# Expert and router products of a two-layer language tower in full float32, the two weight matrices in the two row halves of the TensorE array

## What is computed

```python
flat = _rmsnorm(x, ln2_w).reshape(-1, Cx)                 # 2048 rows of 64
probs = jax.nn.softmax(flat @ router_w.T, axis=-1)        # 8 experts, the best 2 are kept
...
for e in range(NE):                                       # NE = 8, w1, w3: 170 x 64, w2: 64 x 170
    hh = jax.nn.silu(flat @ w1[e].T) * (flat @ w3[e].T)
    out = out + weights[:, e:e + 1] * (hh @ w2[e].T)
```

## Time and profile before

| what | us |
|---|---|
| median of 3 executions (328.81 to 329.77) | 328.85 |
| the profiled execution, own time | 330.29 |
| its span, first to last instruction | 328.5 |
| TensorE busy (89% of the span) | 292.5 |
| VectorE busy (71%) | 233.4 |
| ScalarE busy (45%) | 148.3 |
| GpSimd busy (36%) | 118.0 |
| data moved by transfers | 15.24 MB |

### The profile page before, as it was taken

The page is one execution under the profiler, slowest core; times in us unless marked ns, Lnnn a source line. Parts: engine busy times, 40 slices in busy tenths (PEclk is TensorE's granted clock), DMA queues, the critical chain, the costliest instruction groups (busy, mean ns, idle before and its releaser), DMA issues.

```text
span 328.5 us, 4420 instructions
## 1 busy us (share of the span) xinstructions
PE 292.5 (89%) x1556; PEld 166.5 (51%) x1567; DVE 233.4 (71%) x428; ACT 148.3 (45%) x249; POOL 118.0 (36%) x168
## 2 busy tenths in 40 slices
PE   1649989999989999889999999989999999999873
PEld 1315754753423444467655555555564555557552
DVE  1578788889989778567864687844768677675476
ACT  2113634752566677755547444544533111021283
POOL 5774000331661235301412550430105589930212
PEclk9999999999999999979999999999999999999996
DMA  7958300285000000700000000000000000000001
GB/s 249 335 108 351 167 0 0 42 156 94 3 2 2 2 3 1 257 0 2 1 0 0 3 0 2 0 0 0 3 0 0 2 0 0 1 2 0 0 3 64
DMA packets 6270, 15.24 MB, mean 46 GB/s; under 512 B 1384, under 2 KB 3816, under 8 KB 5608
## 3 DMA queue, kind: packets, MB, share of 16 engines
q1 hardware_dynamic: 5685, 14.41, 14.5%
q0 software_dynamic: 512, 0.53, 0.7%
q10 hardware_dynamic: 51, 0.01, 0.0%
HBM read 12.01 MB, written 0.52 MB: 38 GB/s over the span
## 4 chain that ended last, share of the span: by engine, by line
PE 52%; DVE 9%; POOL 4%; ACT 4%; issue 3%; another core or an unknown queue 0%; POOLq 0%; DVEq 0%; ACTq 0%
PE ps L336 48%; DVE arena L1893 1%; PE ps L837 1%; DVE h L2020 1%; POOL share L600 1%; ACT L1217 1%; PE ps L1110 1%; PE ps L881 1%; POOL share L601 1%; ACT arena L1396 1%; DVE xs L1820 0%; POOL rw L493 0%; DVE h L2069 0%; DVE xc L2081 0%
## 5 line engine op out<-in xcount | busy, mean ns | idle before, releaser
L1759 DVE TENSOR_REDUCE rw<-ps 128x1 f32<-128x512 f32 (+2 forms) x80 | 45.8, 628 | 6.9 <-PE ps L336 6.4
L1336 ACT ACTIVATE arena<-ps 128x1024 f32<-128x1024 f32 (+3 forms) x48 | 37.6, 812 | 23.8 <-PE ps L336 23.3
L336 PE MATMUL ps<-arena 96*128 96x512 bf16 (+7 forms) x192 | 43.1, 327 | 0.5 <-DVE rw L1759 0.2
L336 PE MATMUL ps<-xs,e_hi 128*128 128x512 f32 x96 | 40.5, 422 | 1.0 <-ACT arena L1396 0.8
L1396 ACT ACTIVATE arena<-ps 128x512 f32<-128x512 f32 x48 | 28.5, 597 | 28.1 <-PE ps L336 23.8
L1893 DVE TENSOR_TENSOR arena<-ps,arena 128x512 f32<-128x512 f32 x48 | 32.4, 686 | 11.3 <-ACT arena L1396 9.8
L336 PE MATMUL ps<-xs,e_lo 128*128 128x512 f32 x96 | 37.9, 395 | 0.0
L336 PE MATMUL ps<-bfc_s 128*128 128x512 bf16 (+2 forms) x100 | 27.5, 345 | 1.8 <-DVE xc L1616 1.6
L336 PEld LDWEIGHTS ps<-arena 96*128 96x128 bf16 (+1 forms) x192 | 15.8, 97 | 26.0 <-DVE rw L1759 11.6
L507 POOL TENSOR_SCALAR_AFFINE_SELECT arena<-arena 128x256 f32<-128x256 f32 (+1 forms) x32 | 15.1, 473 | 31.2 <-ACT arena L1336 30.9
L336 PE MATMUL ps<-arena,ew 64*64 64x512 f32 (+1 forms) x128 | 24.2, 609 | 1.7 <-issue 1.4
(11 more groups left out here) (273 smaller groups left out, 513.5 us busy)
## 6 DMA issues: line engine op xcount, KB each, us to landing
arena<-arena SPq DMA_DIRECT2D x24, 96.0 KB, 2.8
w<-wpack SPq DMA_DIRECT2D x1, 2089.5 KB, 10.6
arena<-tm SPq DMA_DIRECT2D x2, 1024.0 KB, 5.8
tables<-epack SPq DMA_DIRECT2D x1, 1540.0 KB, 11.3
arena<-rope SPq DMA_DIRECT2D x1, 1024.0 KB, 13.3
tables<-tu SPq DMA_DIRECT2D x2, 512.0 KB, 3.6
tables<-tk SPq DMA_DIRECT2D x2, 512.0 KB, 6.7
rp<-rpack SPq DMA_DIRECT2D x1, 678.5 KB, 4.3
```

The costliest lines, as they stand in the source:

```text
L336: return nc.tensor.matmul(o, l, r, start=start, stop=stop, **kw)
L1336: nc.scalar.activation(pt[:, n % PT_SLOTS, :, lo:512], ps[:, bank:bank + 2, lo:512], ACT.Exp, scale=HD ** -0.5).then_inc(S("exp_done"), 1)
L1759: V.tensor_reduce(top_view(m, part)[:, at:at + len(heads), i], src, AXX, ALU.max, negate=True).then_inc(S("ring_read"), 1)
```

## The change

It stores the expert and router weights once, as float32 (`e_w`), and `xs` as float32 with the same 64 features in both row halves. A product is one float32 matmul over 64 rows. The one of w1 uses partitions 0 to 63 and rows 0 to 63 of the array, the one of w3 partitions 64 to 127 and rows 64 to 127; they write to the same banks as before. The router's product uses rows 0 to 63. `split_experts` and `low_rows` are gone. `e_w` has its own memory (in the place of the old `e_hi`, whose memory is shared with data of the first attention), so its load now waits for `attn1`, the last use of that data (L1686). `tables` is replaced by two tensors of their own, and the loads of `tu` and `tk` move from behind the attention to right behind that of `e_w`. The wait for `gated` moves ahead of the w1 product.

```diff
@@ the loads, on SP
             sp.dma_start(ew[:], epack[:, NSPLIT:ETOT]).then_inc(ld_e, 16)
-            sp.dma_start(e_raw, epack[:, 0:NSPLIT]).then_inc(ld_e, 16)
+            sp.wait_ge(S("attn1"), 2)
+            sp.dma_start(e_w[:], epack[:, 0:NSPLIT]).then_inc(ld_e, 16)
+            for s in range(2):
+                sp.dma_start(tu_s[:, s], tu[s]).then_inc(ld_u, 16)
+            for s in range(2):
+                sp.dma_start(tk_s[:, s], tk[s]).then_inc(ld_k, 16)
...
-            sp.wait_ge(S("e_low"), E_PARTS)
-            for s in range(2):
-                sp.dma_start(tu_s[:, s], tu[s]).then_inc(ld_u, 16)
-            for s in range(2):
-                sp.dma_start(tk_s[:, s], tk[s]).then_inc(ld_k, 16)
@@ logits and up, on TensorE
-                        mm(o, xs[:, b, j * P:(j + 1) * P], EP(e_hi, "rt", 0, 8), start=True, stop=False)
-                        ins = mm(o, xs[:, b, j * P:(j + 1) * P], EP(e_lo, "rt", 0, 8), start=False, stop=True)
+                        ins = mm(o, xs[0:64, b, j * P:(j + 1) * P], EP(e_w, "rt", 0, 8)[0:64], tile_position=(0, 0))
...
-                rhs = xs[:, b, hf * 512:(hf + 1) * 512]
+                if n >= 3:
+                    pe.wait_ge(S("gated"), n - 2)
                 tile = 3 * pr + n3
                 for m, name in enumerate(("w1", "w3")):
-                    if m == 1 and n >= 3:
-                        pe.wait_ge(S("gated"), n - 2)
-                    o = ps[:, (n % 2, 2 + n % 3)[m]]
-                    mm(o, EP(e_hi, name, tile * P, (tile + 1) * P), rhs, start=True, stop=False)
-                    ins = mm(o, EP(e_lo, name, tile * P, (tile + 1) * P), rhs, start=False, stop=True)
+                    rows = slice(64 * m, 64 * m + 64)
+                    ins = mm(ps[:, (n % 2, 2 + n % 3)[m]], EP(e_w, name, tile * P, (tile + 1) * P)[rows],
+                             xs[rows, b, hf * 512:(hf + 1) * 512], tile_position=(64 * m, 0), skip_group_check=True)
@@ on ScalarE and VectorE
-                nc.scalar.activation(xs[:, b, 512 * a:512 * a + 512], ps[:, bank], ACT.Copy, scale=W("ln2")).then_inc(S("xs_high"), 1)
+                nc.scalar.activation(xs[:, b, 512 * a:512 * a + 512], ps[:, bank], ACT.Copy, scale=W("ln2")).then_inc(S("xs"), 1)
...
-                V.tensor_copy(e_hi[:, at], e_raw[:, at]).then_inc(S("e_high"), 1)
-                V.tensor_tensor(e_lo[:, at], e_raw[:, at], e_hi[:, at].bitcast(F32), ALU.subtract).then_inc(S("e_low"), 1)
...
-                V.scalar_tensor_tensor(out=x, in0=ps[64:P, bank], scalar=W("ln2")[64:P], in1=x.bitcast(F32), op0=ALU.mult,
-                                       op1=ALU.subtract).then_inc(S("xs"), 1)
```

More of the change, by code:

```diff
@@ L71 @@
 SLICES = ((0, 4), (4, 6), (6, 8))
-E_PART = 1027
-E_PARTS = 3
 LAG = 4
@@ L215, in build @@
         arena = sb("arena", [P, 2 * NT * N])
-        tables = sb("tables", [P, 2 * NU * L + NK * L])
+        tu_s = sb("tu_s", [P, 2, NU, L])
+        tk_s = sb("tk_s", [P, 2, NK, L // 2])
         h = sb("h", [P, NT, B, C])
@@ L265, in plan @@
             return views
-        tu_s, tk_s = plan(tables, ([2, NU, L], F32), ([2, NK, L // 2], F32))
-        e_raw = tables[:, 0:NSPLIT]
         qst, kst, yT, pt = plan(arena, ([2, B * NH, 512], BF16), ([B * NKV, N], BF16), ([4, 512], F32), ([PT_SLOTS, 2, 512], F32))
@@ L305, in build @@
         with ExitStack() as experts:
-            e_hi, e_lo, xs = (experts.enter_context(nc.sbuf_tensor(n, sh, F32R)) for n, sh in (
-                ("e_hi", [P, NSPLIT]), ("e_lo", [P, NSPLIT]), ("xs", [P, B, N])))
+            e_w, _, xs = (experts.enter_context(nc.sbuf_tensor(n, sh, F32)) for n, sh in (
+                ("e_w", [P, NSPLIT]), ("e_gap", [P, NSPLIT]), ("xs", [P, B, N])))
         share = sb("share", [P, 2 * NSPLIT + B * N])
@@ L906, in _ @@
             pe.wait_ge(ld_e, 32)
-            pe.wait_ge(S("e_low"), E_PARTS)
             u_at = [0]
@@ L1708, in _ @@
             V.reciprocal(st[:, 4], st[:, 3]).then_inc(S("n2"), 1)
[L1710 to L1714, removed]
-                V.tensor_copy(e_hi[:, at], e_raw[:, at]).then_inc(S("e_high"), 1)
-                dve.wait_ge(S("e_high"), part + 1)
-                V.tensor_tensor(e_lo[:, at], e_raw[:, at], e_hi[:, at].bitcast(F32), ALU.subtract).then_inc(S("e_low"), 1)
             evac(3, S("T2"), 2, S("xT2_hi"), scale=W("ln1"))
@@ L1814, in second_scale @@
                                 ALU.mult).then_inc(S("fhl"), 1)
-            def low_rows(a, b, bank):
-                dve.wait_ge(S("xs_high"), 2 * (1 - a) + b + 1)
-                x = xs[64:P, b, 512 * a:512 * a + 512]
-                V.scalar_tensor_tensor(out=x, in0=ps[64:P, bank], scalar=W("ln2")[64:P], in1=x.bitcast(F32), op0=ALU.mult,
-                                       op1=ALU.subtract).then_inc(S("xs"), 1)
             def table(k, a):
@@ L1859, in add_attention @@
                 step(V.tensor_tensor(half2(h, a), half2(h, a), half2(x1, a), ALU.add))
-            last_top = RING_ORDER.index(("top", len(TOP_UNITS) - 1, 0))
             for n in range(RINGS - 4):
-                if n == last_top:
-                    split_experts(0)
                 if RING_ORDER[n][0] == "o":
@@ L1867, in _ @@
                 ring_item(n)
-                if n in (last_top, last_top + 2):
-                    split_experts((n - last_top) // 2 + 1)
             second_sums(1)
@@ L1874, in _ @@
             ring_item(RINGS - 4)
-            low_rows(1, 0, 3)
-            low_rows(1, 1, 4)
             ring_item(RINGS - 3)
@@ L1944, in _ @@
                         second_scale(0, 1)
[L1945 to L1948, removed]
                     if (n, n3) == (4, 2):
```

## The result

The changed kernel takes 331.44 us (median of 13 executions, 329.76 to 331.95), the kernel before, on the same chip, 329.03 us (13 executions, 328.54 to 330.42). The ratio is 1.006, with an interval of 1.0045 to 1.0075: slower, by 0.45 to 0.75%. The forecast was 330.2 us in a range of 327.0 to 332.8. The profiled execution took 331.44 us with a span of 329.7 us; forecast for it were 331.6 and 329.9.

A forecast was written before the change was run, and what follows sets the result against it. The prediction took TensorE to bound the kernel nearly throughout, over half of the span. Its stretches summed to +1.35 us: 328.85 + 1.35 = 330.2 us for the median, 331.6 for the profiled execution, range 327.0 to 332.8.

The forecast's parts named there:

- The tile: TensorE's expert tiles: two float32 pairs 0.43 us apart, 0.86 us instead of 0.93, 3.3 us less for 48 tiles.
- The two rivals that doubted the overlap: Tile matmuls: same-half weight loads not hidden, 339 to 341 us, chance 0.03; halves not side by side, about 366, chance 0.02.
- The switches: TensorE, pieces between tiles: changing array shape costs an entry of 0.10 us (0.16 with float32 weights) and an exit of 0.21.
- the faster rival: Expert stage: shorter tiles yield 3.3 us and drains hide in TensorE's waits; -2.1 us, 326.8 us, chance 0.20.
- The late gate: Tile (2,1): `gated` now holds the whole tile, which ends at 159.54 instead of 159.13 us, 0.4 us later.
- The sum: From 146 to 233 us, the changes of all stretches add up to +1.35 us.
- the ends of the stretches: Six time sections ending at 166.75, 184.7, 194.0, 205.7, 215 and 233 us; changes about +1.0, -0.2, +0.25, +0.35, +0.1, -0.15.
- What goes at no gain: Removed VectorE work: `split_experts` (5.8 us) covered by TensorE, `low_rows` (4 x 0.76 us) gain between 0 and 1.5, taken as 0.

The follow-up runs named there:

- e8: Changed kernel with eight idle-time matmuls at 138 us, plus VectorE's four `low_rows` instructions put back, results unread but waited for by TensorE; 330.20 us.
- e1: Changed kernel with the wait for `gated` moved back in front of the w3 product alone; 330.94 us, ratio 1.003 to the kernel before.
- e2: Changed kernel with the split's VectorE work (three copies, three subtractions) put back, results unused and not waited for; 331.64 us, ratio 1.0057.
- e4: Changed kernel with the routing-weight spread over rows 0 to 63 only, leaving out the third bfloat16 piece; 329.36 us, ratio 1.0014.
- e7: Kernel before with three float32r products over 64 rows, halves side by side, w_lo x_lo left out; 327.58 us, with eight idle-time matmuls 327.56.
- e3: Changed kernel with the w3 product put in the same row half as w1; 394.03 us, one execution.

## Why the prediction was right, and where it was not

**The tile, right.** 0.43 us a pair, 0.54 from the first to the second behind a full-array piece, 0.52 from the last pair to the spread (233.41 to 233.93). The two rivals that doubted the overlap are out. The Trainium skill, TensorE: Matmul & The Clock Gate, Part 3, The mechanism, says that a load overlaps a running matmul only in another row group. The trace contradicts it at 512 columns as well: bare loads would have made the pairs 0.54 us apart. The forecast said that no row of before shows it at 512 columns; the float32r rows 0.23 us apart, each with a load of its own, did.

**The switches, right.** Entry 0.16 and exit 0.21 less 0.07 make 0.3 us for a lone tile in the forecast, 0.32 in the rows above. The spread over 64 rows took 0.74 us off. That decides against the faster rival, which needed an entry under 0.04 us.

**The late gate, right in size, half right in cause.** The transposes of the earlier trace rows came 0.43 us later, counted from the first tile (forecast 0.4), and the first `down_main` 0.96 later (forecast 1.0). On the profile's own time they stand at 161.39, where they were (forecast 161.8), and 167.28 (forecast 0.9 behind 166.75), since the stage starts 0.44 us earlier. But I put the 0.4 on the moved wait. The working beside it already had the better reason: what is left behind the gate is 1.14 us long and was 0.73. Moved back, the wait saved 0.10 there.

**The sum, a little low.** +1.35 us in the forecast, +1.60 in the stage. By `down_duo` the surplus is spread out: +0.96, +0.83, +0.78, +1.14, +1.52, +1.68, +1.80, +1.59 at its eight starts, against 1.0, 0.8, 1.05, 1.4, 1.5 and 1.35 forecast for the ends of the stretches. At those six ends the measured sum is off by -0.04, -0.02, 0.09, 0.12, 0.18 and 0.24 us. So the 0.24 isn't one term: nothing is missing up to the third start, and from there each stretch costs 0.03 to 0.11 us more than I booked. That the shorter tiles gave back less is one reading; the runs don't separate it from the waits.

**"What goes at no gain", wrong twice.** I took `split_experts` and `low_rows` at 0, and they gave 0.28 and 0.21 us. For the split I had the row in hand: the one wait of TensorE, for GpSimd, 0.2 us. I read it as cover and didn't ask what GpSimd had waited for. For `low_rows` I called three warming matmuls cover. They only fill the time until the first tile may start, and that tile waited for `low_rows` (e8).

**The time: the right forecast of the profiled execution, the wrong median.** 331.6 was forecast for it and 331.44 came, and that is partly luck: the surplus of 0.25 and the two unseen gains of 0.49 nearly cancel, and so do two terms that nobody forecast, the half-clock stretch, 0.28 us dearer in the changed kernel, and the 0.23 us by which its profile was ahead at 121 us already (120.90 against 121.13). For the median I took off 1.44 us, the distance between the profiled execution of before and the median of three others. That distance was the half-clock stretch: two of the three had the lower group's time. In 85 executions the kernel before has a median of 329.89 us and not 328.85. So the 1.2 us by which the result lies above 330.2 are mostly a question of how many executions have the stretch, and without it the change costs about 1 us, 0.3%.

**What stays open.** Whether the changed kernel has the stretch more often at all. 10 of its 13 executions are in the upper group against 45 of 85 of before, and with so few that can be chance; in e1, e2 and e4, built on it, it is 7 of 10, 5 of 7 and 4 of 10. The idle time is the same, 2.1 us. That filling it removes both upper groups is shown; what tips a single execution is not.

## What to carry to other kernels

Splitting an array into row halves pays by the time of a row times their number, and the switch of the shape is paid at every piece of other shape between: count the pieces before the columns. Here float32 halves (two rows of 0.43) had 0.07 us a tile to give against 0.2 to 0.3 a switch, and float32r halves (three of 0.23, one product of four left out) 0.24. When a wait of the bounding engine goes to an engine that seems idle, ask what that one was held up by before calling the work beside it covered. And if execution times fall into two groups, look for an idle time of TensorE ahead of a half-clock stretch, before pricing a change by medians. In e7 two groups were left when it was filled.

## What the runs showed of the hardware that I had not expected

- GpSimd waited out whole instructions of VectorE. A 16-column subtraction on GpSimd took 1.20 us, and a cast of 16 columns 0.59, while VectorE worked through 1027 columns; alone they take 0.21 and 0.20. The subtraction of before ended at 123.75, VectorE's at 123.68. The Trainium skill, SBUF — State Buffer, SBUF: two separate sides, states that the port pair shared by the two is locked for a whole instruction and the loser blocks. The trace agrees for the subtraction, which has two inputs on both engines.
- The clock was at 1.2 GHz for 48 us while TensorE was busy for 47.5 of them, on 64-row work in one half (e3). The same kind of work kept 2.4 GHz from 217 to 296 us of that run (busy 78.0 of 79 us), and work in both halves did in the whole stage of the changed kernel. What made the difference is open.
- Eight matmuls of 512 columns in 2.1 us of idle time, with a result nobody reads, are worth 0.9 us in the median of the kernel before (329.89 to 328.95) and 1.5 in the changed one (331.44 to 329.93, not measured side by side).
